# Mixture-of-experts stage of a two-layer transformer kernel: routing weights sent to DRAM and read back over each expert's partitions, in place of TensorE's spreads

## The chip, the cores and the metric

The kernel runs on one core of one Trainium2 chip. The metric is the device time of one execution in microseconds; the number given for a kernel is the median of several executions. A profile is one execution recorded by the hardware profiler. Engines are named as in the profile: PE (TensorE, with PEld for its weight loads), DVE (VectorE), ACT (ScalarE), POOL (GpSimd) and SP (SyncE, which here only issues transfers).

## The reference

32 samples of 256 tokens with 128 features pass through two layers, each an attention block and a feed-forward block, with a layer norm and a per-sample scale, shift and gate around each. The change lies in the feed-forward block of the first layer, a mixture of experts:

```python
def relu2(x): return jnp.square(jax.nn.relu(x))
# router: 16 experts in 4 groups; the 2 best groups by the sum of their 2 best scores,
# then the 4 best experts in them
scores = jax.nn.sigmoid(x2 @ gate_w.T)
sc = scores + bias_e
...
topk_w = topk_w / (topk_w.sum(-1, keepdims=True) + 1e-20) * 2.5
combine = zeros((T, 16)).at[rows, topk_idx].add(topk_w)
def body(acc, inp):
    wu, wd, cw = inp                       # wu (64, 128), wd (128, 64), cw (T,)
    return acc + cw[:, None] * (relu2(x2 @ wu.T) @ wd.T)
routed = scan(body, 0, (up_w, down_w, combine.T))
shared = relu2(x2 @ shared_up.T) @ shared_down.T      # inner size 256
out = routed + shared
```

## The kernel before

The program is a series of stages: setup, first attention, experts (`moe`), second attention, second feed-forward. A barrier stands between two stages. All 32 samples' tokens stay in SBUF (`x`). The experts' stage takes 16 runs (`RUNS`) of two samples each, so 512 tokens (`W`) in 4 tiles of 128.

In a run the inner features are taken in ten blocks `u` of 128 (`IT`): blocks 0 and 1 are the shared expert, blocks 2 to 9 are two routed experts each (j = u - 2, experts 2j and 2j+1, 64 partitions each). For a block, PE multiplies the normalised tokens `hT` into `pU` (`pe_up`), ACT takes the relu into `r` and the square into `q` (into `a` for the shared expert), DVE multiplies `q` by the routing weights (`dve_weigh`) into `a`, and PE multiplies `a` back and adds up in `pD` (`pe_down`). The weight of a token for an expert must stand on all 64 partitions of that expert. Before, this is done by PE: DVE writes the weights [token, expert] as two f16 halves (high part and rest) into `cwp`, PE transposes them (`pe_turn_weights`), ACT copies them to `cwT` (`act_take_weights`), and for each routed block PE multiplies `cwT` by a matrix of zeros and ones, `sel`, into `pC` (`pe_spread`), which `dve_weigh` reads.

The routing itself is a chain on DVE: `dve_scores`, `dve_groups`, `dve_group_ranks`, `dve_chosen`, `dve_weights`, laid out between the `dve_weigh` of the run before. Around it stand `dve_normalise`, PE's transposes of the normalised tokens (`pe_front`), ACT's scale and shift (`act_modulate`), the router's product (`pe_route`) and ACT's exponential (`act_exp`). At a run's end ACT applies the gate (`act_gate`), PE transposes back (`pe_back`) and DVE adds to `x` (`dve_add`).

The order of the work on every engine is written out by hand in one loop per engine; each engine works strictly in that order, and waits on semaphores whose counts are written out too. SP issues in this stage only the weight loads of the last stage (`ahead(sp)`), and is idle after that.

Of the kernel before, what the change touches and what calls it, by code (L numbers as in the profile page):

```python
# [7 lines left out]
F32 = mybir.dt.float32  # L8
# [924 lines left out]
def moe(nc, c, weights, ahead):  # L933


    with ExitStack() as ctx:
# [4 lines left out]
        def sem(name):  # L941
# [7 lines left out]
        RSTEPS = 32  # L949
# [3 lines left out]
        sel = sb('sel', [P, RT, P], F16)  # L953
        lt4 = sb('lt4', [P, NG, NG])
        xn = sb('xn', [P, T4, D])
        hT = [sb(f'hT{k}', [D, W]) for k in range(2)]
        s, cw = (sb(x, [P, T4, E]) for x in ('s', 'cw'))
# [7 lines left out]
        cwp = sb('cwp', [P, T4, P], F16)  # L965
        cwT = [sb(f'cwT{k}', [P, W], F16) for k in range(2)]
# [33 lines left out]
        def pe_route(pe, n):  # L1000
            pe.wait_ge(s_hT, n + 1)
            if n >= 1:
                pe.wait_ge(s_cw, n)
            for t in range(T4):
                last = pe.matmul(pR[:, t * E:(t + 1) * E], hT[n % 2][:, t * P:(t + 1) * P], gT[:, :], start=True, stop=True)
            last.then_inc(s_lg, 1)

        def pe_turn_weights(pe, n):
            pe.wait_ge(s_rt, RSTEPS * (n + 1))
            out = pR[:, BANK // 2:BANK].bitcast(F16)  # L1010
            for t in range(T4):
                last = pe.transpose(out[:, t * P:(t + 1) * P], cwp[:, t, :], c.id16[:, :])
            last.then_inc(s_cT, 1)

        def pe_up(pe, n, u):
            if u == 0:
                pe.wait_ge(s_hT, n + 1)
            if n or u >= 2:
                pe.wait_ge(s_r, IT * n + u - 1)
            t = weights_of(u)  # L1020
            pe.matmul(pU[u % 2][:, :], uT[:, t * P:(t + 1) * P], hT[n % 2][:, :], start=True, stop=True).then_inc(s_up, 1)  # L1021

        def pe_spread(pe, n, u):
            j = u - ST
            if j == 0:
                pe.wait_ge(s_cw, n + 1)
            if n or j >= 2:
                pe.wait_ge(s_a, RT * n + j - 1)
            pe.matmul(pC[j % 2][:, :], sel[:, j, :], cwT[n % 2][:, :], start=True, stop=True).then_inc(s_cb, 1)
# [20 lines left out]
        def _(pe):  # L1050
# [11 lines left out]
            pe.wait_ge(s_k, 4)  # L1062
            for n in range(-1, RUNS + 1):
                if 0 <= n < RUNS:
                    pe_up(pe, n, 0)
                if 0 <= n - 1 < RUNS:
                    pe_down(pe, n - 1, 7)
                if 0 <= n < RUNS:
                    pe_up(pe, n, 1)
                if 0 <= n - 1 < RUNS:  # L1070
                    pe_down(pe, n - 1, 8)
                if 0 <= n < RUNS:
                    pe_turn_weights(pe, n)
                    pe_up(pe, n, 2)
                    pe_spread(pe, n, 2)
                if 0 <= n - 1 < RUNS:
                    pe_down(pe, n - 1, 9)
                if 0 <= n + 1 < RUNS:
                    pe_front(pe, n + 1)
                if 0 <= n < RUNS:  # L1080
                    pe_up(pe, n, 3)
                    pe_spread(pe, n, 3)
                    pe_down(pe, n, 0)
                    pe_up(pe, n, 4)
                    pe_spread(pe, n, 4)
                    pe_down(pe, n, 1)
                if 0 <= n + 1 < RUNS:
                    pe_route(pe, n + 1)
                if 0 <= n < RUNS:
                    pe_up(pe, n, 5)  # L1090
                    pe_spread(pe, n, 5)
                if 0 <= n - 1 < RUNS:
                    pe_back(pe, n - 1)
                if 0 <= n < RUNS:
                    pe_down(pe, n, 2)
                    for u in range(6, IT):
                        pe_up(pe, n, u)
                        pe_spread(pe, n, u)
                        pe_down(pe, n, u - 3)
# [62 lines left out]
        def dve_weights(dve, n):  # L1162
            base = RSTEPS * n
            dve.wait_ge(s_rt, base + 25)
            dve.scalar_tensor_tensor(cw[:, :, :], rep[:, :, 0:E], TAKEN, s[:, :, :], ALU.is_equal, ALU.mult).then_inc(s_rt, 1)
# [31 lines left out]
        def _(dve):  # L1197
# [6 lines left out]
            for n in range(-1, RUNS + 1):  # L1204
                if 0 <= n - 1 < RUNS:
                    dve_weigh(dve, n - 1, 9)
                if 0 <= n < RUNS:
                    dve_weights(dve, n)
                if 0 <= n + 1 < RUNS:
                    dve_normalise(dve, n + 1)  # L1210
# [8 lines left out]
                if 0 <= n + 1 < RUNS:  # L1219
                    dve_scores(dve, n + 1)  # L1220
# [4 lines left out]
                if 0 <= n + 1 < RUNS:  # L1225
                    dve_groups(dve, n + 1)
# [4 lines left out]
                if 0 <= n + 1 < RUNS:  # L1231
                    dve_group_ranks(dve, n + 1)
# [4 lines left out]
                if 0 <= n + 1 < RUNS:  # L1237
                    dve_chosen(dve, n + 1)
# [3 lines left out]
        def act_modulate(act, n):  # L1242
            if n >= 2:
                act.wait_ge(s_up, IT * (n - 1))
            act.wait_ge(s_xT, n + 1)
            for m in range(S2):
                last = act.activation(hT[n % 2][:, m * N:(m + 1) * N], pX[:, m * N:(m + 1) * N], ACT.Identity, scale=c.mod[:, 0, 4, n * S2 + m:n * S2 + m + 1], bias=c.mod[:, 0, 3, n * S2 + m:n * S2 + m + 1])
            last.then_inc(s_hT, 1)

        def act_exp(act, n):  # L1250
            act.wait_ge(s_lg, n + 1)
            if n >= 1:
                act.wait_ge(s_rt, RSTEPS * (n - 1) + 26)
# [19 lines left out]
        def act_take_weights(act, n):  # L1273
            act.wait_ge(s_cT, n + 1)
            if n >= 2:
                act.wait_ge(s_cb, RT * (n - 1))
            act.activation(cwT[n % 2][:, :], pR[:, BANK // 2:BANK].bitcast(F16), ACT.Copy).then_inc(s_cw, 1)

# [9 lines left out]
        def _(act):  # L1288
            for n in range(-1, RUNS + 1):
                if 0 <= n < RUNS:  # L1290
# [3 lines left out]
                    act_take_weights(act, n)  # L1294
# [7 lines left out]
                if 0 <= n + 1 < RUNS:  # L1302
                    act_modulate(act, n + 1)
# [5 lines left out]
                if 0 <= n + 1 < RUNS:  # L1309
                    act_exp(act, n + 1)  # L1310
# [7 lines left out]
        def _(gp):  # L1318
            gp.memset(sel[:, :, :], 0.0).then_inc(s_k, 1)
            gp.memset(lt4[:, :, :], 1.0).then_inc(s_k, 1)  # L1320
            for k in range(2):
                gp.wait_ge(s_k, 2 + k)
                m = sel[:, :, :].rearrange('r t (x i) -> r t x i', i=EI)
                gp.affine_select(out=m, in_=m, compare_op=ALU.not_equal, fill=1.0, base=k * E, pattern=[[2, RT], [1, 2], [0, EI]], channel_multiplier=-1).then_inc(s_k, 1)
# [3 lines left out]
            gp.memset(cwp[:, :, 2 * E:], 0.0).then_inc(s_km, 1)  # L1328
# [765 lines left out]
```

## Time and profile before

| | us |
|---|---|
| median of 3 executions | 2152.71 (2152.59 to 2153.12) |
| profiled execution, its own time | 2151.95 |
| span of its profile | 2150.1 |
| PE busy | 2047.2 (95%) |
| DVE busy | 1650.3 (77%) |
| ACT busy | 1438.3 (67%) |
| POOL busy | 618.3 (29%) |

The profile's times count from the start of the span; "busy" is the time in which an engine executed an instruction, overlaps counted once. The experts' stage has its first matmul at 1002.3 us and its last at 1354.45 us. A wait is put down to the instruction that ended last before it.

### The profile page before, as it was taken

Reading aid. Unit: us, or ns where it says so; the run is one execution under the profiler, and the core shown is the slowest. Engines: PE = TensorE matmul, PEld = TensorE weight load, DVE = VectorE, ACT = ScalarE, POOL = GpSimd, SP = SyncE. Lnnn points to the kernel's source line nnn. Section 1 sums busy time; section 2 is a strip of 40 time slices with the busy share of each in tenths; the row PEclk is TensorE's granted clock in tenths of the full one; section 3 lists DMA queues with packets and bytes.
Section 4 is the critical chain, followed back from the end, with each engine's and each line's share of the span. In section 5 each row is a group of like instructions: output and inputs, shape, how many; then the busy total and the mean of one; then the engine's idle time right before and its main releaser. Section 6 shows DMA issues by size and latency. Waiting matters only on the chain. (4 is left out here: it accounts for less than half of the span.)

```text
span 2150.1 us, 40463 instructions
## 1 busy us (share of the span) xinstructions
PE 2047.2 (95%) x14885; PEld 1372.3 (64%) x14885; DVE 1650.3 (77%) x4015; ACT 1438.3 (67%) x1931; POOL 618.3 (29%) x862
## 2 busy tenths in 40 slices
PE   3899999999999999997999999799999996999998
PEld 1577777777777777775444444577777773444443
DVE  3888888888888888874566665577777776999997
ACT  1687877778887777873666666466666663555554
POOL 1345444544544454552000000133333331000000
PEclk9999999999999999997999999899999997999999
DMA  5000000000000000001000000000000000000000
GB/s 165 21 21 21 21 11 21 21 21 21 21 21 11 21 21 21 21 21 55 1 0 1 1 1 1 1 2 2 2 2 2 2 2 1 10 16 11 15 11 20
DMA packets 32834, 35.30 MB, mean 16 GB/s; under 512 B 6864, under 2 KB 26496, under 8 KB 32640
## 3 DMA queue, kind: packets, MB, share of 16 engines
q1 hardware_dynamic: 32640, 32.73, 5.8%
q8 instruction: 120, 1.97, 0.4%
q14 instruction: 74, 0.61, 0.1%
HBM read 11.75 MB, written 4.19 MB: 7 GB/s over the span
## 5 line engine op out<-in xcount | busy, mean ns | idle before, releaser
L864 POOL TENSOR_SCALAR_AFFINE_SELECT pr<-pr 128x512 f32<-128x512 f32 x256 | 202.2, 813 | 370.7 <-ACT pr L795 370.7
L422 PE MATMUL a_pO<-va,pr 128*128 128x66 f32 x2048 | 304.6, 272 | 1.9 <-POOL pr L864 1.5
L422 PEld LDWEIGHTS a_pO<-va,pr 128*128 128x128 f32 x2048 | 273.7, 193 | 18.9 <-issue 15.4
L1628 ACT ACTIVATE c_pr<-c_pS 128x1536 f32<-128x1536 f32 x128 | 186.0, 1453 | 119.3 <-PE c_pS L1440 119.3
L1683 POOL TENSOR_SCALAR_AFFINE_SELECT c_pr<-c_pr 128x512 f32<-128x512 f32 x256 | 158.0, 641 | 265.4 <-DVE c_pr L1548 265.4
L761 ACT ACTIVATE sq<-a_pW 128x512 f32<-128x512 f32 x192 | 114.4, 597 | 145.4 <-PE a_pW L363 142.7
L789 ACT ACTIVATE th<-a_pS 128x1536 f32<-128x1536 f32 x128 | 185.9, 1453 | 30.1 <-PE a_pS L407 29.6
L423 PE MATMUL a_pO<-va,pr 128*128 128x66 f32 x1024 | 199.0, 276 | 0.0
L795 ACT ACTIVATE pr<-th 128x1536 f32<-128x1536 f32 x128 | 190.5, 1488 | 3.1
L407 PE MATMUL a_pS<-qs,k 128*128 128x512 f16 (+1 forms) x1024 | 187.3, 326 | 0.9 <-issue 0.9
L1548 DVE TENSOR_SCALAR c_pr<-c_pr 128x1536 f32<-128x1536 f32 x128 | 122.6, 958 | 78.4 <-ACT c_pr L1628 78.4
L1021 PE MATMUL b_pU<-b_hT,b_uT 128*128 128x512 f32 x320 | 168.8, 610 | 0.0
L1039 PE MATMUL b_pD<-b_a,b_dT 128*128 128x512 f32 x320 | 163.1, 593 | 0.0
L407 PEld LDWEIGHTS a_pS<-qs,k 128*128 128x128 f16 x1024 | 98.7, 98 | 99.7 <-issue 35.9
L1187 DVE TENSOR_TENSOR b_a<-b_q,b_pC 128x512 f32<-128x512 f32 x128 | 87.8, 686 | 96.1 <-ACT b_q L1271 96.0
L1258 ACT ACTIVATE b_r<-b_pU 128x512 f32<-128x512 f32 x160 | 95.4, 596 | 95.6 <-PE b_pU L1021 95.6
L423 PEld LDWEIGHTS a_pO<-va,pr 128*128 128x128 f32 x1024 | 156.6, 193 | 0.0
L872 POOL TENSOR_TENSOR as<-on 128x128 f32<-128x128 f32 x256 | 116.6, 466 | 109.7 <-PE a_pW L444 95.0
L643 POOL TENSOR_TENSOR qp<-qg,qp 128x1024 f16<-128x1024 f32 x64 | 136.7, 2137 | 25.2 <-ACT qp L771 25.2
L582 DVE TENSOR_TENSOR qg<-a_pW,a_gam 128x512 f32<-128x512 f32 x192 | 131.4, 685 | 10.5 <-ACT sq L761 7.9
L634 DVE RECIPROCAL rl<-a_pO 128x4 f32<-128x4 f32 x256 | 45.0, 176 | 120.5 <-PE a_pO L423 120.5
L363 PE MATMUL a_pW<-a_wq,hT 128*128 128x512 f32 x256 | 125.7, 615 | 1.3 <-DVE qs L651 0.7
(259 smaller groups left out, 4509.1 us busy)
## 6 DMA issues: line engine op xcount, KB each, us to landing
k<-k SPq DMA_DIRECT2D x64, 256.0 KB, 3.6
x<-in_L_attn_tokens_dram SPq DMA_DIRECT2D x8, 512.0 KB, 6.8
out_dram<-x SPq DMA_DIRECT2D x16, 256.0 KB, 2.3
d_h<-in_L_ffn_h_w_dram SPq DMA_DIRECT2D x2, 1024.0 KB, 7.4
wmod<-in_L_wmod_dram SPq DMA_DIRECT2D x2, 384.0 KB, 4.0
d_w<-in_L_ffn_w_w_dram SPq DMA_DIRECT2D x3, 256.0 KB, 3.2
a_wq<-in_L_attn_Wq_dram SPq DMA_DIRECT2D x1, 512.0 KB, 7.1
a_wkv<-in_L_attn_Wkv_dram SPq DMA_DIRECT2D x1, 512.0 KB, 6.9
```

The costliest lines, as they stand in the source:

```text
L407: last = pe.matmul(out, kk[:, h // G2, keys * P:(keys + 1) * P], qs[k][:, h:h + G2, keys * P:N], start=first, stop=not first)
L422: pe.matmul(out, w[:, hh * N + t * P:hh * N + (t + 1) * P], v[:, 0, p, :], start=True, stop=t == 0)
L423: last = pe.matmul(out, w[:, HPG * N + hh * P:HPG * N + (hh + 1) * P], v[:, 1, p, :], start=False, stop=True)
L582: dve.tensor_tensor(qg[n % 2][:, t, cols], pW[BANK_OF[m]][:, :], gam[:, cols], ALU.mult).then_inc(s_qg, 1)
L643: eng.tensor_tensor(to[:, t, :, DH:2 * DH], x.rearrange('p (h d) -> p h d', d=DH), to[:, t, :, 0:DH], ALU.subtract).then_inc(done, 1)
L789: act.activation(th[:, :], pS[:, :], ACT.Tanh, scale=1.0 / SOFTCLAMP).then_inc(s_th, 1)
L795: act.activation(pr[g % 2][:, :], th[:, :], ACT.Exp, scale=SOFTCLAMP * DH ** (-0.5)).then_inc(s_pr, 1)
L864: last = gp.affine_select(out=part, in_=part, compare_op=ALU.is_ge, fill=0.0, base=0, pattern=[[0, HPG], [1, P]], channel_multiplier=-1)
L1021: pe.matmul(pU[u % 2][:, :], uT[:, t * P:(t + 1) * P], hT[n % 2][:, :], start=True, stop=True).then_inc(s_up, 1)
L1039: pe.matmul(pD[:, :], dT[:, t * D:(t + 1) * D], a[(IT * n + u) % 4][:, :], start=u == 0, stop=u == IT - 1).then_inc(s_dn, 1)
L1628: act.activation(pr[g][:, :, :], pS[:, :, 0:N + P], ACT.Exp, scale=float(1.0 / np.sqrt(np.float32(DQ)))).then_inc(s_ex, 1)
L1683: last = gp.affine_select(out=part, in_=part, compare_op=ALU.is_ge, fill=0.0, base=0, pattern=[[0, HPG], [1, P]], channel_multiplier=-1)
```

## The change

The spread by PE is taken out. In its place:

- DVE writes the weights as f32 into `cwp` (32 columns for each tile of tokens, 16 of them used) and transposes them with its own transpose, in blocks of 32 by 32, into `cwT`: block row k holds the experts of the tokens 32k to 32k+31 of every tile.
- SP, in a loop over the runs, waits for `cwT` and for the reads of the run before, issues 4 transfers that write `cwT` to a buffer in DRAM (`by_expert`, ordered by expert), waits until they have landed, and issues 8 transfers that read the rows of two experts each back into `cwB[n % 2][:, j, :]`, each expert's row of 512 weights on 64 partitions. Each of the 8 has a semaphore of its own, `s_cw[j]`, and `dve_weigh` waits for it.
- The routing of a run is done one run earlier: PE's `pe_front` and `pe_route`, ACT's `act_modulate` and `act_exp` and DVE's routing chain now stand for run n+2 where they stood for n+1. `hT` has three buffers, `s` two.
- `pU` has four banks of PSUM instead of two (the two of `pC` are free), so `pe_up` may run further ahead of ACT.

The core of the diff:

```diff
+        cwp, cwT = (sb(x, [P, T4, SQ]) for x in ('cwp', 'cwT'))
+        cwB = [sb(f'cwB{k}', [P, RT, W]) for k in range(2)]
+        by_expert = nc.dram_tensor('b_by_expert', (E, T4, P // SQ, SQ), F32, kind='Internal').ap()
...
         @block.sync
         def _(sp):
             ahead(sp)
+            for n in range(RUNS):
+                sp.wait_ge(s_cT, n + 1)
+                if n >= 1:
+                    for j in range(RT):
+                        sp.wait_ge(s_cw[j], 16 * n)
+                for j in range(P // SQ):
+                    sp.dma_start(by_expert[:, :, j, :], cwT[SQ * j:SQ * j + E, :, :]).then_inc(s_cd, 16)
+                sp.wait_ge(s_cd, 16 * P // SQ * (n + 1))
+                if n >= 2:
+                    sp.wait_ge(s_a, RT * (n - 1))
+                rows = by_expert.rearrange('(j y) t k r -> j y (t k r)', y=2)
+                for j in range(RT):
+                    sp.dma_start(cwB[n % 2][:, j, :], rows[j].unsqueeze(1).broadcast_to((2, EI, W))).then_inc(s_cw[j], 16)
...
-        def pe_turn_weights(pe, n):
-            pe.wait_ge(s_rt, RSTEPS * (n + 1))
-            out = pR[:, BANK // 2:BANK].bitcast(F16)
-            for t in range(T4):
-                last = pe.transpose(out[:, t * P:(t + 1) * P], cwp[:, t, :], c.id16[:, :])
-            last.then_inc(s_cT, 1)
...
-        def pe_spread(pe, n, u):
-            ...
-            pe.matmul(pC[j % 2][:, :], sel[:, j, :], cwT[n % 2][:, :], start=True, stop=True).then_inc(s_cb, 1)
...
-            dve.scalar_tensor_tensor(cw[:, :, :], cw[:, :, :], ROUTED, tot[:, :].unsqueeze(2).broadcast_to((P, T4, E)), ALU.mult, ALU.mult).then_inc(s_rt, 1)
+            dve.scalar_tensor_tensor(cwp[:, :, 0:E], cw[:, :, :], ROUTED, tot[:, :].unsqueeze(2).broadcast_to((P, T4, E)), ALU.mult, ALU.mult).then_inc(s_rt, 1)
             dve.wait_ge(s_rt, base + 30)
             if n >= 1:
-                dve.wait_ge(s_cT, n)
-            dve.tensor_copy(cwp[:, :, 0:E], cw[:, :, :]).then_inc(s_rt, 1)
-            dve.wait_ge(s_rt, base + 31)
-            dve.tensor_tensor(cwp[:, :, E:2 * E], cw[:, :, :], cwp[:, :, 0:E], ALU.subtract).then_inc(s_rt, 1)
+                dve.wait_ge(s_cd, 16 * P // SQ * n)
+            dve.transpose(cwT[:, :, :].rearrange('p t r -> p (t r)'), cwp[:, :, :].rearrange('p t e -> p (t e)')).then_inc(s_cT, 1)
 
         def dve_weigh(dve, n, u):
             j = u - ST
             dve.wait_ge(s_sq, IT * n + u + 1)
-            dve.wait_ge(s_cb, RT * n + j + 1)
+            dve.wait_ge(s_cw[j], 16 * (n + 1))
             if n or u >= 4:
                 dve.wait_ge(s_dn, IT * n + u - 3)
-            dve.tensor_tensor(a[(IT * n + u) % 4][:, :], q[j % 4][:, :], pC[j % 2][:, :], ALU.mult).then_inc(s_a, 1)
+            dve.tensor_tensor(a[(IT * n + u) % 4][:, :], q[j % 4][:, :], cwB[n % 2][:, j, :], ALU.mult).then_inc(s_a, 1)
```

The first place is PE in the middle of the stage, from one run to the next. Before, its rows there are (L1021 is `pe_up`, L1039 `pe_down`, L1012 `pe_turn_weights`, L1029 `pe_spread`, L997 `pe_front`, L1005 `pe_route`):

```order
L1039 MATMUL b_pD<-b_a,b_dT 128x512
L1012 MATMUL b_pR<-id,b_cwp 128x128 x4
L1021 MATMUL b_pU<-b_hT,b_uT 128x512
L1029 MATMUL b_pC<-b_cwT,b_sel 128x512
L1039 MATMUL b_pD<-b_a,b_dT 128x512
L997 MATMUL b_pX<-id,b_xn 128x128 x4
L1021 MATMUL b_pU<-b_hT,b_uT 128x512
L1029 MATMUL b_pC<-b_cwT,b_sel 128x512
```

Of the change the same place reads (L1030 is `pe_up`, L1040 `pe_down`, L1013 `pe_front`):

```order
L1040 MATMUL b_pD<-b_a,b_dT 128x512
L1030 MATMUL b_pU<-b_hT,b_uT 128x512
L1040 MATMUL b_pD<-b_a,b_dT 128x512
L1013 MATMUL b_pX<-id,b_xn 128x128 x4
L1030 MATMUL b_pU<-b_hT,b_uT 128x512
```

The spreads and the transposes of the weights are gone, and nothing stands in their place on PE.

The second place is SP behind the weight loads of the last stage, of the change (before, SP has no row here); a row's brackets name the semaphores that it waits for, and the names are the written and the read tensor:

```order
L1700 DMA d_w3s<-in_L_ffn_w_s_dram 128x1
L997 DMA b_by_expert<-b_cwT 64x1x32 [waits b_cT]
L997 DMA b_by_expert<-b_cwT 64x1x32 x3
L1003 DMA b_cwB<-b_by_expert 128x1x512 [waits b_cd]
L1003 DMA b_cwB<-b_by_expert 128x1x512 x7
L997 DMA b_by_expert<-b_cwT 64x1x32 [waits b_cw4,b_cw3,b_cw5,b_cw2,b_cw6,b_cw1,b_cw7,b_cw0,b_cT]
L997 DMA b_by_expert<-b_cwT 64x1x32 x3
L1003 DMA b_cwB<-b_by_expert 128x1x512 [waits b_cd]
```

A run's four writes wait for all eight reads of the run before, and its eight reads wait for its four writes, so the runs' transfers do not overlap.

The third place is DVE at the stage's start, of the change (L1165 to L1171 end `dve_weights`, L1105 is `dve_scores`): behind the first run's weights stands the whole routing of the second run.

```order
L1165 RECIPROCAL b_tot<-b_tot 128x4 [waits b_rt]
L1167 SCALAR_TENSOR_TENSOR b_cwp<-b_cw,b_tot 128x4x16 [waits b_rt]
L1171 STREAM_TRANSPOSE b_cwT<-b_cwp 128x128 [waits b_rt]
L1105 TENSOR_SCALAR b_s<-b_s 128x64 [waits b_ex]
L1107 RECIPROCAL b_s<-b_s 128x64 [waits b_rt]
```

Before, the normalising of the second run's tokens (L103) and the first `dve_weigh` (L1187) stood right behind the first run's weights:

```order
L1173 SCALAR_TENSOR_TENSOR b_cw<-b_cw,b_tot 128x64 [waits b_rt]
L1177 CAST b_cwp<-b_cw 128x4x16 [waits b_rt]
L1179 TENSOR_TENSOR b_cwp<-b_cw,b_cwp 128x4x16 [waits b_rt]
L103 TENSOR_SCALAR b_xn<-x,mv,rs 128x128 [waits b_xT]
L103 TENSOR_SCALAR b_xn<-x,mv,rs 128x128 x3
L1187 TENSOR_TENSOR b_a<-b_q,b_pC 128x512 [waits b_cb,b_sq] x2
```

A second routing chain has come between the first run's weights and the work that follows them.

## Rows read from the trace of the kernel before

**Rows 1.** Stretches: length, then each engine's busy us, PE's clock, DMA share, GB/s

```profile
1110.00:1130.00 20.00, 20.00 (x67) 9.84 (x66) 13.13 (x58) 13.04 (x26) 0.00 (x0) 1.00 0.00 0
1130.00:1150.00 20.00, 20.00 (x68) 9.78 (x66) 13.09 (x58) 13.04 (x25) 0.00 (x0) 1.00 0.01 2
1360.00:1400.00 40.00, 33.22 (x330) 24.96 (x331) 23.05 (x47) 22.59 (x25) 12.00 (x22) 0.85 0.00 1
```

**Rows 2.** Timeline of PE, mid-stage: start us, length us, then the instructions merged

```profile
1113.69 1.02 PE L1021 MATMUL b_pU<-b_hT,b_uT 128*128 128x512 f32 x2
1114.55 0.38 PE L1029 MATMUL b_pC<-b_cwT,b_sel 128*128 128x512 f16 x1
1114.77 1.02 PE L1039 MATMUL b_pD<-b_a,b_dT 128*128 128x512 f32 x2
...
1123.14 1.02 PE L1021 MATMUL b_pU<-b_hT,b_uT 128*128 128x512 f32 x2
1124.00 1.02 PE L1039 MATMUL b_pD<-b_a,b_dT 128*128 128x512 f32 x2
1124.86 0.39 PE L1012 MATMUL b_pR<-id,b_cwp 128*128 128x128 f16 x4
1125.08 1.08 PE L1021 MATMUL b_pU<-b_hT,b_uT 128*128 128x512 f32 x2
1125.99 0.38 PE L1029 MATMUL b_pC<-b_cwT,b_sel 128*128 128x512 f16 x1
...
1145.80 0.39 PE L1012 MATMUL b_pR<-id,b_cwp 128*128 128x128 f16 x4
```

**Rows 3.** Groups of the stage by line and shape: busy us, mean ns, idle before

```profile
L1187 DVE TENSOR_TENSOR b_a<-b_q,b_pC 128x512 f32<-128x512 f32 x128 | 87.8, 686 | 96.1 <-ACT b_q L1271 96.0
...
L1029 PE MATMUL b_pC<-b_cwT,b_sel 128*128 128x512 f16 x128 | 48.8, 381 | 0.0
```

**Rows 4.** Timeline at the stage's start, with the last step of the first run's weights

```profile
1012.63 0.20 DVE L1111 TENSOR_SCALAR b_s<-b_s 128x64 f32<-128x64 f32 x1 [4.07 <-ACT b_s L1254]
...
1018.89 0.23 DVE L1179 TENSOR_TENSOR b_cwp<-b_cw,b_cwp 128x64 f16<-128x64 f32 x1
...
1021.81 1.06 PE L997 MATMUL b_pX<-id,b_xn 128*128 128x128 f32 x4
```

**Rows 5.** Timeline at the stage's end: the last weighing and the gate

```profile
1351.14 0.69 DVE L1187 TENSOR_TENSOR b_a<-b_q,b_pC 128x512 f32<-128x512 f32 x1 [1.16 <-ACT b_q L1271]
...
1353.56 0.84 ACT L1284 ACTIVATE b_og<-b_pD,mod 128x256 f32<-128x256 f32 x2 [2.45 <-PE b_pD L1039]
```

**Rows 6.** Timeline of SP in the first attention: two transfers issued

```profile
525.69 0.46 SPq L306 DMA_DIRECT2D k<-k  x1
526.20 0.60 SPq L307 DMA_DIRECT2D k<-k  x1
```

**Rows 7.** DMA issues: count, KB each, median us from issue to landing

```profile
k<-k SPq DMA_DIRECT2D x64, 256.0 KB, 3.6
out_dram<-x SPq DMA_DIRECT2D x16, 256.0 KB, 2.3
...
b_gn<-in_L_ffn_gate_w_dram SPq DMA_DIRECT2D x1, 8.0 KB, 2.7
```

**Rows 8.** DMA of 554 to 562 us, holding two k transfers of 64 x 4 KB

```profile
GB/s 0 0 0 0 0 0 0 0 164 205 266 246 123 246 61 246 430 389 246 0 0 0 0 0 0 0 0 0 0 0 0 0 0 0 0 0 0 0 0 0
DMA packets 160, 0.52 MB, mean 66 GB/s; under 512 B 32, under 2 KB 32, under 8 KB 160
## 3 DMA queue, kind: packets, MB, share of 16 engines
q1 hardware_dynamic: 160, 0.52, 26.0%
```

**Rows 9.** DMA of 1007 to 1007.5 us, packets of 2 KB alone

```profile
q1 hardware_dynamic: 66, 0.14, 84.2%
```

**Rows 10.** DMA of 1012 to 1012.5 us, packets of 2 KB alone

```profile
DMA packets 97, 0.20 MB, mean 397 GB/s; under 512 B 0, under 2 KB 0, under 8 KB 97
...
q1 hardware_dynamic: 97, 0.20, 106.0%
```

**Rows 11.** The instructions of pe_up: ns min/median/max, first and last start

```profile
L1021 PE MATMUL b_pU<-b_hT,b_uT x320: 592/592/1201, 1012.2 to 1349.2; 128*128 128x512 f32 x160
```

More of the change, by code:

```diff
@@ L948, in moe @@
         ROW = E + EG
-        RSTEPS = 32
+        RSTEPS = 30
+        SQ = 32
         HIGH, TAKEN = 3.0e38, -3.0e38
@@ L952, in moe @@
         uT, dT, gT = (sb('uT', [D, IT * P]), sb('dT', [P, IT * D]), sb('gT', [D, E]))
-        sel = sb('sel', [P, RT, P], F16)
         lt4 = sb('lt4', [P, NG, NG])
         xn = sb('xn', [P, T4, D])
-        hT = [sb(f'hT{k}', [D, W]) for k in range(2)]
-        s, cw = (sb(x, [P, T4, E]) for x in ('s', 'cw'))
+        hT = [sb(f'hT{k}', [D, W]) for k in range(3)]
+        s = [sb(f's{k}', [P, T4, E]) for k in range(2)]
+        cw = sb('cw', [P, T4, E])
         sc, mk, rep = (sb(x, [P, T4, ROW]) for x in ('sc', 'mk', 'rep'))
@@ L1002, in pe_route @@
             if n >= 1:
-                pe.wait_ge(s_cw, n)
+                pe.wait_ge(s_ex, n)
             for t in range(T4):
-                last = pe.matmul(pR[:, t * E:(t + 1) * E], hT[n % 2][:, t * P:(t + 1) * P], gT[:, :], start=True, stop=True)
+                last = pe.matmul(pR[:, t * E:(t + 1) * E], hT[n % 3][:, t * P:(t + 1) * P], gT[:, :], start=True, stop=True)
             last.then_inc(s_lg, 1)
-        def pe_turn_weights(pe, n):
-            pe.wait_ge(s_rt, RSTEPS * (n + 1))
-            out = pR[:, BANK // 2:BANK].bitcast(F16)
-            for t in range(T4):
-                last = pe.transpose(out[:, t * P:(t + 1) * P], cwp[:, t, :], c.id16[:, :])
-            last.then_inc(s_cT, 1)
         def pe_up(pe, n, u):
@@ L1017, in pe_up @@
                 pe.wait_ge(s_hT, n + 1)
[L1018 to L1019 removed]
+            if n or u >= 4:
+                pe.wait_ge(s_r, IT * n + u - 3)
             t = weights_of(u)
[L1021 to L1029 removed]
+            pe.matmul(pU[(IT * n + u) % 4][:, :], uT[:, t * P:(t + 1) * P], hT[n % 3][:, :], start=True, stop=True).then_inc(s_up, 1)
         def pe_down(pe, n, u):
@@ L1061, in _ @@
             pe.wait_ge(s_taken, len(turns))
-            pe.wait_ge(s_k, 4)
-            for n in range(-1, RUNS + 1):
+            for n in range(-2, RUNS + 1):
                 if 0 <= n < RUNS:
@@ L1203, in _ @@
             dve.wait_ge(s_km, 4)
-            for n in range(-1, RUNS + 1):
+            for n in range(-2, RUNS + 1):
                 if 0 <= n - 1 < RUNS:
                     dve_weigh(dve, n - 1, 9)
-                if 0 <= n < RUNS:
-                    dve_weights(dve, n)
                 if 0 <= n + 1 < RUNS:
-                    dve_normalise(dve, n + 1)
+                    dve_weights(dve, n + 1)
+                if n == -2:
+                    dve_normalise(dve, 0)
+                    dve_normalise(dve, 1)
+                elif 0 <= n < RUNS - 2:
+                    dve_normalise(dve, n + 2)
                 if 0 <= n < RUNS:
@@ L1288, in _ @@
         def _(act):
-            for n in range(-1, RUNS + 1):
+            for n in range(-2, RUNS + 1):
                 if 0 <= n < RUNS:
@@ L1318, in _ @@
         def _(gp):
-            gp.memset(sel[:, :, :], 0.0).then_inc(s_k, 1)
             gp.memset(lt4[:, :, :], 1.0).then_inc(s_k, 1)
[L1321 to L1324, printed above, removed]
+            gp.wait_ge(s_k, 1)
             gp.affine_select(out=lt4[:, :, :], in_=lt4[:, :, :], compare_op=ALU.is_gt, fill=0.0, base=0, pattern=[[1, NG], [-1, NG]], channel_multiplier=0).then_inc(s_km, 1)
```

82 lines of the change are left out of this document (34 added, 48 removed).

## The prediction

> **What bounds the kernel now.** I read three views in this order. The stretches of the experts' stage come first: in two windows of 20 us PE is busy for all 20.00 us at a granted clock of 1.00, which is 2.4 GHz, while DVE and ACT have some 13 us of work and the DMA engines none [rows 1]. The reader is to see that every other engine has slack and transfers have the whole machine to themselves. The timeline of PE shows what a run is made of: the same row, the transposes of the weights, starts at 1124.86 and at 1145.80 us, so a run takes 20.94 us, and 16 runs make 335 us of the 2150 [rows 2]. Third, the groups: DVE's weighing waits 96.0 us in the stage for ACT's squares, behind which PE stands again [rows 3]. So the stage goes at PE's pace, and whatever leaves PE is gained, as long as nothing else takes longer than PE's run.
>
> **What leaves PE.** A spread takes a slot of 1114.77 - 1114.55 = 0.22 us between a `pe_up` and a `pe_down` [rows 2]; its mean of 381 ns overlaps the next matmul [rows 3]. Eight make 1.74 us. The transposes of the weights take 0.22 us (1124.86 to 1125.08), and the `pe_up` behind them has a slot of 0.91 us where others have 0.86 (1123.14 to 1124.00) [rows 2]. Together 2.0 us of a run, so PE's run becomes 18.94 us. ACT loses one copy, DVE a cast and a subtraction for one transpose of 128x128; neither is near 18.94 us.
>
> **What comes in its place.** SP's loop is a closed chain, and I price one turn of it.
> - Four writes: SP needs 0.46 to 0.60 us for an issue [rows 6], so the fourth goes out 1.6 us after the first. It moves little; small or DRAM-bound transfers land 2.3 to 2.7 us after issue [rows 7]; I take 2.3. That is 3.9 us, and no read may start before.
> - Start of the reads: the two k transfers of rows 7 need 3.6 us each for 64 packets, of which data is some 2 us in the burst of rows 8; about 1.5 us are latency. Sum so far 5.4 us.
> - Eight reads: each writes 128 rows of 2 KB, 256 KB, so 1024 packets and 2.1 MB a run. How long they take hangs on how many of the 16 DMA engines carry them.
>
> That last point decides everything. What the trace shows of sharing out: the two k transfers have 64 rows of 4 KB each on both sides, and left 128 packets of data and 32 small ones, 16 for each transfer, while their burst reached 430 GB/s [rows 8]. So a transfer whose outer dimension is 64 has its rows dealt to all 16 engines, with one closing packet on each. The new reads differ in one thing: the destination has 128 partitions outside, but the source is written as 2 rows, each repeated 64 times, so its outer dimension is 2. If engines are dealt equal pieces of the outer dimension of both sides, there are only 2 equal pieces to deal, each of 64 packets, and all eight reads come to lie on two engines. No row of the trace has a transfer with an outer dimension under 16, so the rows can't show it; I choose this reading, because the closing packets show that the deal is made by whole shares of the instruction's rows, and the share here can't be finer than the source's two rows without cutting through the repeat.
>
> The Trainium skill states this as a rule (DMA: Bandwidth & Descriptors, "Why a DMA increments its semaphore by 16 and not by 1"): the number of engines is the largest up to 16 that divides both sides' slowest dimension, and on SP's queue it is the lowest-numbered ones that work; its "Rules for kernel authors" warns of an outermost dimension under 16. By that rule each read runs on engines 0 and 1 alone, the same two every time. Rows 8 agree for 64 (16 closing packets); no run here shows it for 2 so far.
>
> **The price of two engines.** Packets of 2 KB alone: 97 of them in 0.5 us took 106.0% of 16 engines, 0.5 x 16 x 1.06 / 97 = 87 ns each, and by rate 397 / 16 = 24.8 GB/s, 83 ns [rows 10]. I take 85 ns. Each of two engines has 8 x 64 = 512 packets a run: 43.5 us. A turn is 5.4 + 43.5 = 48.9 us, against 18.94 of PE's. PE's own run may even fall to half clock for its idling (`pe_up` takes 592 ns at full and up to 1201 at half clock [rows 11]): 2 x 18.94 = 37.9 us still hides beneath 48.9. The double buffer doesn't help, since this is throughput; nor does choosing the weights a run ahead, which covers one turn's latency and not a queue that grows.
> - First write: the weights of the first run are done at 1019.1 us before [rows 4]; one step less and the transpose leave about 1019.0.
> - Last read landed: 1019.0 + 16 x 48.9 = 1801.4 us. The last weighing, at 1351.14 us before [rows 5], waits for it: +450.3.
> - Tail and next stage: the last `pe_down`, the transposes back and the first matmuls of the second attention now run at the lower clock from the start (that stretch has 0.85 before [rows 1]): I put 3 us, chosen between 0 and 6.
>
> Sum +453 us. The profiled execution took 2151.95 us by its own time, 0.8 below the median 2152.71, so 2152.7 + 453 = **2606 us**.
>
> **Bounds.** The fastest slice of the k burst, 430 GB/s, is 26.9 GB/s an engine, 76 ns for 2 KB [rows 8]: turn 44.3, kernel 2533. In another half microsecond 66 packets took 84.2%, 102 ns [rows 9]: turn 57.6, kernel 2746. The k packets as a whole, 26.0% of 16 engines in 8 us for 128 of 4 KB, are 130 ns for 2 KB [rows 8]: turn 72, kernel 2976; their engines also waited for one another's SBUF rows, so I hold it for an outer end. That 64 packets read the same row of DRAM has no row at all; it could cost or save. The transpose on DVE and its wait for the writes are hidden either way: in a turn of 48.9 us DVE has 13.
>
> **Rivals.**
> 1. *All sixteen engines share each read, or the pairs differ from read to read: faster.* Then the reads need 1024 x 85 / 16 = 5.4 us, the turn 10.8 us, under 18.94, and PE stays the bound. Gain 16 x 2.0 = 32.0 us. Against it stands the start: DVE's chain from scores to weights takes 6.4 us (1012.63 to 1019.1) [rows 4], and now a second one stands before the normalising of the run that `pe_front` needs. `pe_front`, at 1021.81 before, starts at about 1019.0 + 6.1 + 1.1 = 1026.2, and PE's low clock lasts longer: together 5.5 us; 0.9 us of spreads were hidden in that start already; back come 1.3 us, since one transpose and routing more lies in the idle start. 32.0 - 5.5 - 0.9 + 1.3 = 26.9: **2126 us**. For it: the 430 GB/s burst. Against it: the source's form. It decides as soon as a turn is below 18.94 us, that is from about 7 engines on (5.4 + 1024 x 0.085 / 7 = 17.8).
> 2. *Sixteen engines, but the reads land one after another*: 3.9 + 8 x 3.6 [rows 7] = 32.7 us a turn, 1019 + 523 = 1542, +191: **2344 us**. Against it: two k transfers issued 0.5 us apart [rows 6] were both over in the one burst of rows 8.
> 3. *Two engines, and rereading one DRAM row makes a packet dearer*: at 102 ns 2746 us, in the first case's own range.
>
> **How the numbers follow.** Two engines, with any price of a packet, 0.84: its own range 2520 to 2870 (packets of 74 to 117 ns, the bounds above without the outermost) holds 95 in 100 of it. Sixteen or changing pairs 0.12, of which almost nothing comes out within 0.2% of before, some 4 us, which is about what a measurement of this kernel can tell from no change. One after another 0.04. Time 2606 us, that of the likeliest; range 2520 to 2870, which holds 0.84 x 0.95 = 0.80 of all and so need not reach the others. Faster 0.12, same 0.01, slower 0.87.
>
> **What the changed profile would show.** In the experts' stage a DMA share near 2/16 = 0.11 to 0.13 without a gap, about 43 GB/s; DVE's weighing released by the reads of `cwB` and not by ACT, most of DVE's idle time in front of it; PE busy well under 90% and its clock at 0.50 for most of the stage; the reads' landing times spread up to over 40 us, and SP waiting for them at the first write. The stage some 785 us long. A share of 0.3 in bursts of 6 to 10 us with PE still at 20.00 of 20 would show rival 1; reads that land at 3.6 us steps, rival 2. The prediction is wrong if engines are dealt single rows whatever the form of the source; it is off in size if a packet on a lonely engine takes another time than in a burst of sixteen.

## The result, and the profile after

The changed kernel takes 2589.36 us (2588.71 to 2589.5) against 2152.65 us of before measured beside it: a ratio of 1.2028, 95% interval 1.2007 to 1.2049, slower by 437 us. Forecast were 2606 us, in a range of 2520 to 2870.

The page of the changed kernel: first busy time of the engines (share of the span, instructions), then the span in 40 slices with PE's clock, the DMA share and GB/s, and one row of its costliest groups.

```profile
PE 2172.5 (84%) x14693; PEld 1385.4 (54%) x14693; DVE 1653.1 (64%) x3999; ACT 1436.0 (55%) x1915; POOL 615.6 (24%) x859
...
PE   3999999999999997655566656564999999799999
...
PEclk9999999999999996888877777776999999899999
DMA  4100010001000001111111111110000000000000
GB/s 137 25 18 18 17 25 18 18 18 26 17 17 18 19 24 52 46 46 42 46 45 44 46 43 45 46 42 32 2 2 2 2 2 2 1 9 17 13 13 17
...
L1179 DVE TENSOR_TENSOR b_a<-b_q,b_cwB 128x512 f32<-128x512 f32 x128 | 88.6, 692 | 524.1 <-DMA b_cwB<-b_by_expert 265.9
```

The experts' stage now fills slices 16 to 28. The DMA row holds a flat 1 in slices 16 to 27, a tenth of the sixteen engines, with 42 to 52 GB/s and never more. DVE's weighing waits 524 us, where it waited 96 us behind ACT [rows 3]; 265.9 us of it are put down to the reads, and 220.5 us to "issue", which names no cause, but at the same pace of 5.20 us as the rows below show. A stretch in the stage is to be set beside [rows 1]; under it, of ten microseconds in the middle of a run's reads, the DMA view:

```profile
1200.00:1250.00 50.00, 29.43 (x59) 11.37 (x57) 13.53 (x57) 14.03 (x26) 0.00 (x0) 0.81 0.12 45
```

```profile
DMA packets 250, 0.50 MB, mean 50 GB/s; under 512 B 4, under 2 KB 4, under 8 KB 250
## 3 DMA queue, kind: packets, MB, share of 16 engines
q1 hardware_dynamic: 250, 0.50, 13.1%
```

13.1% of sixteen engines is 2.1 engines; 16 x 10 x 0.131 / 250 = 84 ns for a packet. PE is busy for 29 us in 50, where it was for 20 in 20. SP's timeline gives the turn of the loop, DVE's the pace of the reads:

```profile
1021.57 2.58 SPq L997 DMA_DIRECT2D b_by_expert<-b_cwT  x4
1025.38 30.17 SPq L1003 DMA_DIRECT2D b_cwB<-b_by_expert  x8
1069.45 2.51 SPq L997 DMA_DIRECT2D b_by_expert<-b_cwT  x4
1073.19 29.82 SPq L1003 DMA_DIRECT2D b_cwB<-b_by_expert  x8
1117.20 2.50 SPq L997 DMA_DIRECT2D b_by_expert<-b_cwT  x4
```

```profile
1229.85 0.69 DVE L1179 TENSOR_TENSOR b_a<-b_q,b_cwB 128x512 f32<-128x512 f32 x1 [4.52 <-DMA b_cwB<-b_by_expert]
1235.06 0.69 DVE L1179 TENSOR_TENSOR b_a<-b_q,b_cwB 128x512 f32<-128x512 f32 x1 [4.52 <-DMA b_cwB<-b_by_expert]
1240.26 0.69 DVE L1179 TENSOR_TENSOR b_a<-b_q,b_cwB 128x512 f32<-128x512 f32 x1 [3.91 <-issue]
...
1788.29 0.69 DVE L1179 TENSOR_TENSOR b_a<-b_q,b_cwB 128x512 f32<-128x512 f32 x1 [4.41 <-issue]
```

From write to write a turn is 47.8 us (47.6 to 48.4, mean 47.9): 3.8 us until the first read goes out, 8 reads at 5.20 us each (41.6), and a remainder of 2.4 us for the start of the first read and the landing of the last. The last row is the stage's last weighing; it stood at 1351.14 us [rows 5], so it comes 437.2 us later, and the span grew by 437.5.

### The profile page after: what moved, and what is told of

Read it like the earlier page. It is cut to its first block and busy times, and to the rows that moved or that the text cites. A ratio compares the mean times of both kernels' runs of the same rounds, so it can differ in the third digit from the quotient of the medians.

```text
span 2587.6 us, 40277 instructions
## 1 busy us (share of the span) xinstructions
PE 2172.5 (84%) x14693; PEld 1385.4 (54%) x14693; DVE 1653.1 (64%) x3999; ACT 1436.0 (55%) x1915; POOL 615.6 (24%) x859
## 5 line engine op out<-in xcount | busy, mean ns | idle before, releaser
L1040 PE MATMUL b_pD<-b_a,b_dT 128*128 128x512 f32 x320 | 236.1, 829 | 271.5 <-DVE b_a L1179 271.5
L1179 DVE TENSOR_TENSOR b_a<-b_q,b_cwB 128x512 f32<-128x512 f32 x128 | 88.6, 692 | 524.1 <-DMA b_cwB<-b_by_expert 265.9
L1040 PEld LDWEIGHTS b_pD<-b_a,b_dT 128*128 128x128 f32 x320 | 64.7, 240 | 426.7 <-DVE b_a L1179 400.3
L1030 PE MATMUL b_pU<-b_hT,b_uT 128*128 128x512 f32 x320 | 225.3, 798 | 0.0
```

Of the source, the lines that this page charges most:

```text
L1030: pe.matmul(pU[(IT * n + u) % 4][:, :], uT[:, t * P:(t + 1) * P], hT[n % 3][:, :], start=True, stop=True).then_inc(s_up, 1)
L1040: pe.matmul(pD[:, :], dT[:, t * D:(t + 1) * D], a[(IT * n + u) % 4][:, :], start=u == 0, stop=u == IT - 1).then_inc(s_dn, 1)
```

## The experiments

Each is the changed kernel with one edit unless said otherwise. Experiments 3 and 6 to 9 are one execution each, so a few us in their times mean little; ratios are to before, measured beside them. Rival A is that rereading one DRAM row is what costs; rival B that SP's queue is the limit and not the engines.

**1. One expert a read.** The same bytes and the same repeats, but both outer dimensions are 64.

```diff
-                    sp.dma_start(cwB[n % 2][:, j, :], rows[j].unsqueeze(1).broadcast_to((2, EI, W))).then_inc(s_cw[j], 16)
+                    for y in range(2):
+                        sp.dma_start(cwB[n % 2][y * EI:(y + 1) * EI, j, :], rows[j][y:y + 1].broadcast_to((EI, W))).then_inc(s_cw[j], 16)
```

The waits on `s_cw` count in 32 instead of 16.

> Edit: each read of 128 partitions is cut into two of 64, one expert's row repeated 64 times, so that the outer dimension is 64 on both sides; the same 2.1 MB a run and the same rereading of each DRAM row 64 times. Theory (a transfer is dealt to as many engines as both outer dimensions can be cut into equally; 2 in the changed kernel): all 16 engines work, a turn of SP's loop is 3.8 us of writes, 16 issues of about 0.5 us and 2 to 3 us to the last landing, 14 to 15 us, below PE's 18.9; PE is the bound again, its run 18.94 us, kernel 2126 us (2120 to 2135), DMA share near 0.3. Rival A (rereading one DRAM row is what is slow, whatever the number of engines): the same row is read as often, so the turn stays near 47.8 us and the kernel at 2589. Rival B (SP's queue can hold only so many transfers, and each costs its 5.2 us): 16 transfers make it no better, 2589 or slower.

Measured: 2125.44 us (2124.34 to 2128.02), 0.9878 of before (0.9862 to 0.9895). The same data arrive, each DRAM row still read 64 times, from the same queue in twice as many transfers, and 464 us are gone: rivals A and B both fall. In its profile, two rows of PE's timeline, one run apart, then the DMA view of 1200 to 1219 us, then SP's timeline:

```profile
1217.83 0.60 PE L1014 MATMUL b_pX<-id,b_xn 128*128 128x128 f32 x4
1236.79 0.60 PE L1014 MATMUL b_pX<-id,b_xn 128*128 128x128 f32 x4
```

```profile
DMA packets 1641, 2.14 MB, mean 113 GB/s; under 512 B 616, under 2 KB 616, under 8 KB 1640
## 3 DMA queue, kind: packets, MB, share of 16 engines
q1 hardware_dynamic: 1640, 2.13, 37.1%
```

```profile
1018.79 2.56 SPq L997 DMA_DIRECT2D b_by_expert<-b_cwT  x4
1022.58 10.08 SPq L1004 DMA_DIRECT2D b_cwB<-b_by_expert  x16
1034.94 2.49 SPq L997 DMA_DIRECT2D b_by_expert<-b_cwT  x4
```

PE's run is 18.96 us (18.94 by the prediction's working). A turn of SP's loop is 16.2 us, of which 10.1 go into issuing 16 transfers: 2.8 us below PE's run; 14 to 15 us were expected, and 10.8 us in the prediction's rival with eight reads.

**2. Two reads a run.**

```diff
-                rows = by_expert.rearrange('(j y) t k r -> j y (t k r)', y=2)
-                for j in range(RT):
-                    sp.dma_start(cwB[n % 2][:, j, :], rows[j].unsqueeze(1).broadcast_to((2, EI, W))).then_inc(s_cw[j], 16)
+                rows = by_expert.rearrange('(j y) t k r -> y j (t k r)', y=2)
+                for y in range(2):
+                    sp.dma_start(cwB[n % 2][y * EI:(y + 1) * EI, :, :], rows[y:y + 1].broadcast_to((EI, RT, W))).then_inc(s_cw[y], 16)
```

> Edit: two reads a run instead of eight, each of 64 partitions with all eight rows of one half (even or odd experts), outer dimension 64 on both sides, 1 MB each; each weighing waits for both. Theory (engines by the outer dimension): both reads on 16 engines, 1024 packets of 81 ns over 16 engines are 5.2 us, the turn 3.8 + 0.5 + 5.2 + 2.4, about 12 us; PE the bound, 2126 us, at most 2 us beside the first experiment; SP has 14 issues fewer, which costs nothing either way as SP has time. Rival A (rereading a row): 2589. Rival B (each transfer costs 5.2 us): the turn would be 3.8 + 2.4 + 10.4 = 16.6 us, also under 18.9, so this run doesn't test B; the first does.

Measured: 2131.62 us, 0.9905 (0.989 to 0.9919), 6 us more than the first experiment where at most 2 were expected. DVE's timeline at the start and the DMA view of 1200 to 1219 us:

```profile
1038.23 2.50 DVE L1180 TENSOR_TENSOR b_a<-b_q,b_cwB 128x512 f32<-128x512 f32 x4 [9.58 <-DMA b_cwB<-b_by_expert]
```

```profile
DMA packets 1378, 2.15 MB, mean 113 GB/s; under 512 B 352, under 2 KB 352, under 8 KB 1376
## 3 DMA queue, kind: packets, MB, share of 16 engines
q1 hardware_dynamic: 1376, 2.13, 54.2%
```

The first weighing needs both megabytes and waits 9.58 us for them, 1.96 us of which reach PE; from first matmul to last weighing the stage is 2.0 us longer than in the first experiment (325.7 against 323.7). Another 2.7 us of the 5.5 us between the two profiles' spans lie ahead of the stage: its first matmul came at 1004.26 us here and at 1001.59 in the first experiment, in work that the edit doesn't touch. The last 0.8 us lie behind it, unexplained. And a packet costs more: 54.2% of sixteen engines for the bytes that took 37.1% there.

**3. Four outer pieces instead of two.**

```diff
-        by_expert = nc.dram_tensor('b_by_expert', (E, T4, P // SQ, SQ), F32, kind='Internal').ap()
+        by_expert = nc.dram_tensor('b_by_expert', (E, 2, T4, P // SQ, SQ), F32, kind='Internal').ap()
...
+                    for d in range(2):
+                        sp.dma_start(by_expert[:, d, :, j, :], cwT[SQ * j:SQ * j + E, :, :]).then_inc(s_cd, 16)
...
-                rows = by_expert.rearrange('(j y) t k r -> j y (t k r)', y=2)
+                rows = by_expert.rearrange('(j y) d t k r -> j (y d) (t k r)', y=2)
...
-                    sp.dma_start(cwB[n % 2][:, j, :], rows[j].unsqueeze(1).broadcast_to((2, EI, W))).then_inc(s_cw[j], 16)
+                    sp.dma_start(cwB[n % 2][:, j, :], rows[j].unsqueeze(1).broadcast_to((4, EI // 2, W))).then_inc(s_cw[j], 16)
```

> Edit: each expert's row is written to DRAM twice (8 small writes a run instead of 4) and each read takes 4 rows, each repeated 32 times: the outer dimension of the source is 4 instead of 2, everything else of the reads as in the changed kernel. Theory (engines by the outer dimension): 4 engines, 32 packets each a read, 2.6 us a read; turn 8 x 0.6 + 1.8 for the writes, 8 x 2.6 = 20.8 for the reads, 2.4 latency, 29.8 us; PE still waits; kernel 2589 - 16 x (47.8 - 29.8) = 2301 us; DMA share in a read burst 4/16 = 0.25. Rival A (rereading one DRAM row): each row is reread half as often; if that were the cost the reads would fall to something between 41.6 and 20.8 us a run but the DMA share would stay at 0.12. Rival B (a transfer's fixed price of 5.2 us): 47.8 + 2.4, kernel about 2627.

Measured: 2274.87 us. DVE's weighings come 2.60 us apart, half of 5.20, and in 1082 to 1100 us the DMA view says four engines, 25.6% of sixteen:

```profile
1088.69 0.69 DVE L1180 TENSOR_TENSOR b_a<-b_q,b_cwB 128x512 f32<-128x512 f32 x1 [1.88 <-DMA b_cwB<-b_by_expert]
1091.30 0.69 DVE L1180 TENSOR_TENSOR b_a<-b_q,b_cwB 128x512 f32<-128x512 f32 x1 [1.92 <-DMA b_cwB<-b_by_expert]
```

```profile
q1 hardware_dynamic: 872, 1.74, 25.6%
```

The kernel is 26 us under the forecast because it takes 4.7 us from the first of the eight small writes to the first read, and not 6.6: the turn is 28.1 us on average instead of 29.8. The share of 25.6% speaks against rival A, which had 0.12, and a transfer's fixed price (rival B) is excluded once more.

**4. Reads in the first two runs only.** Fourteen runs weigh with old routing weights.

```diff
-            for n in range(RUNS):
+            for n in range(2):
                 sp.wait_ge(s_cT, n + 1)
...
-                dve.wait_ge(s_cd, 16 * P // SQ * n)
+                dve.wait_ge(s_cd, 16 * P // SQ * min(n, 2))
...
-            dve.wait_ge(s_cw[j], 16 * (n + 1))
+            dve.wait_ge(s_cw[j], 16 * min(n + 1, 2))
```

> Edit: SP makes its writes and reads only for the first two runs; later runs weigh with what stands in the two buffers, so the routing weights of 14 of the 16 runs are left wrong (the work of all engines but the DMA queue is unchanged). Theory: shows PE's run of 18.94 us without any transfer beside it and the price of the start: the first two turns are 47.8 us each on two engines, so runs 0 and 1 end at about 1021.6 + 95.6 = 1117, the other 14 go at PE's 18.94 us: about 1117 + 14 x 18.94 + 5 = 1387, 401 less than 1788: kernel about 2188 us. If transfers slowed PE or DVE in SBUF, the steady run here would be shorter than in the first experiment; I expect the same within 0.05 us.

Measured: 2179.8 us, 1.0127 of before (1.0112 to 1.0142), 8 us under the forecast. PE's timeline in its steady part, without a transfer beside it:

```profile
1216.86 0.60 PE L1013 MATMUL b_pX<-id,b_xn 128*128 128x128 f32 x4
1235.82 0.60 PE L1013 MATMUL b_pX<-id,b_xn 128*128 128x128 f32 x4
```

18.96 us again. The 2.1 MB a run of the first experiment take nothing measurable from PE, DVE or ACT: from 1200 to 1219 us DVE is busy 13.26 us with them and 13.30 without, ACT 13.65 and 13.65.

**5. The start mended**, on top of the first experiment.

```diff
                 if n == -2:
                     dve_normalise(dve, 0)
                     dve_normalise(dve, 1)
-                elif 0 <= n < RUNS - 2:
+                elif n == -1:
+                    dve_normalise(dve, 2)
+                elif 1 <= n < RUNS - 2:
                     dve_normalise(dve, n + 2)
```

> Edit: the first experiment (one expert a read, 16 engines), and DVE normalises the third run's tokens before the second run's routing and not behind it. Theory (rival 1 of the prediction as it now stands: 16 x 2.0 us gained, some 5.5 us lost at the start, where PE waited 4.72 us for these tokens at half clock): PE's transposes of them start near 1021 instead of 1026.04 us and the clock rises earlier; DVE's first weighing stays at 1026.1 and its result is wanted a little later, so 4 to 5 us come back: 2121 us (2118 to 2124) against 2125.4. Rival: the first weighing at 1026.1 is late then and the wait only moves from the tokens to PE's third product with the down weights: at most 1 us gained.

Measured: 2121.39 us (2118.56 to 2123.15), 0.985 of before (0.9836 to 0.9863), the fastest kernel of the study; the interval just touches the first experiment's. Within the stage it is plain. The first matmul, the transposes of the third run's tokens, and the last weighing, of the first experiment:

```profile
1001.59 2.37 PE L1060 MATMUL b_pU<-id,b_un 128*128 128x128 f32 x10 [5.13 <-PEq L246]
...
1026.04 1.12 PE L1014 MATMUL b_pX<-id,b_xn 128*128 128x128 f32 x4 [4.72 <-DVE b_xn L103]
...
1325.29 0.69 DVE L1180 TENSOR_TENSOR b_a<-b_q,b_cwB 128x512 f32<-128x512 f32 x1 [0.94 <-ACT b_q L1267]
```

and of the fifth:

```profile
1004.78 2.37 PE L1060 MATMUL b_pU<-id,b_un 128*128 128x128 f32 x10 [5.13 <-PEq L246]
...
1023.24 0.60 PE L1014 MATMUL b_pX<-id,b_xn 128*128 128x128 f32 x4
...
1029.54 1.12 PE L1041 MATMUL b_pD<-b_a,b_dT 128*128 128x512 f32 x2 [0.51 <-DVE b_a L1180]
...
1321.28 0.69 DVE L1180 TENSOR_TENSOR b_a<-b_q,b_cwB 128x512 f32<-128x512 f32 x1 [0.94 <-ACT b_q L1269]
```

The transposes come 18.5 us into the stage instead of 24.5, without a wait and already at full clock (0.60 us for four, not 1.12), and the stage is 7.2 us shorter. Only 4 us show in the time, since this execution entered the stage 3.2 us later. The rival's wait is there, but small: PE waits 0.51 us for the first weighing.

**6. The same reads from POOL's queue.** The read loop stands in POOL's program, with the same waits.

```diff
+            for n in range(RUNS):
+                gp.wait_ge(s_cd, 16 * P // SQ * (n + 1))
+                if n >= 2:
+                    gp.wait_ge(s_a, RT * (n - 1))
+                rows = by_expert.rearrange('(j y) t k r -> j y (t k r)', y=2)
+                for j in range(RT):
+                    gp.dma_start(cwB[n % 2][:, j, :], rows[j].unsqueeze(1).broadcast_to((2, EI, W))).then_inc(s_cw[j], 16)
```

> Edit: the changed kernel with its eight reads of outer dimension 2 unchanged, but issued by POOL instead of SP (POOL is idle in this stage). Theory (what is dealt equally is the outer dimension, and which engines get it belongs to the queue): the Trainium skill says that from POOL's queue a transfer on few engines goes to consecutive engines from a cursor that moves on, and from SP's to the lowest-numbered. Then each read still takes 64 packets of 81 ns, 5.2 us, but the eight run side by side on 16 engines: turn 3.8 + about 1 us an issue, 8 + 5.2 + 2.4, some 19 us, kernel 2126 to 2170, DMA share in a burst over 0.5. Rival (the shape limits to the same two engines from any queue): turn 47.8 or more, kernel 2589 or more, DMA share 0.12.

Measured: 2165.59 us. The DMA view of 1100 to 1140 us:

```profile
DMA  8742001000344588999999751000100143557999
GB/s 152 142 128 75 4 0 17 10 7 0 12 65 101 125 198 193 195 169 165 218 179 166 190 121 45 0 0 10 15 8 0 22 57 89 121 170 194 195 173 149
...
q0 software_dynamic: 7621, 3.79, 49.9%
...
b_cwB<-b_by_expert POOLq DMA_DIRECT2D x16, 256.0 KB, 11.8
```

Reads of the very same form now reach 218 GB/s with all engines at work in the middle of the burst. So the two outer pieces alone don't tie them to one pair; the pair is that of SP's queue. The turn is 21.3 us on average, above PE's 18.96 and above the 19 expected, and the price of a read is why. On POOL's queue (q0) the same bytes take twice the engine time: 16 x 40 x 0.499 = 319 us for 3.79 MB are 173 ns for 2 KB, the queue's many small packets included, against 84 ns on SP's queue. 64 rows at that price on one engine are 11 us, and a read lands 11.8 us after its issue. With 3.8 us for the writes and seven issues of 0.8 us ahead of the last read that gives 21.1 us.

**7. Odd reads from ACT's queue.**

```diff
-                for j in range(RT):
+                for j in range(0, RT, 2):
                     sp.dma_start(cwB[n % 2][:, j, :], rows[j].unsqueeze(1).broadcast_to((2, EI, W))).then_inc(s_cw[j], 16)
...
+        def act_reads(act, n):
+            act.wait_ge(s_cd, 16 * P // SQ * (n + 1))
+            if n >= 2:
+                act.wait_ge(s_a, RT * (n - 1))
+            rows = by_expert.rearrange('(j y) t k r -> j y (t k r)', y=2)
+            for j in range(1, RT, 2):
+                act.dma_start(cwB[n % 2][:, j, :], rows[j].unsqueeze(1).broadcast_to((2, EI, W))).then_inc(s_cw[j], 16)
```

> Edit: the changed kernel with its reads unchanged, the four of even j issued by SP and the four of odd j by ACT at the end of the run before. Theory (two engines, the lowest-numbered ones from either queue): the 512 packets an engine stay, turn 47.8, kernel 2575 to 2640; ACT may wait while it issues, hidden beneath the reads. Rival B (SP's queue, not the engines, is what passes one read in 5.2 us): two queues pass two at once, turn 3.8 + 4 x 5.2 + 2.4 = 27 us, kernel 2256, DMA share 0.25 in a burst.

Measured: 2593.95 us. Two queues (q1 is SP's, q10 ACT's) share what one had, in 1100 to 1150 us:

```profile
q1 hardware_dynamic: 861, 1.12, 6.2%
q10 hardware_dynamic: 541, 1.09, 5.9%
```

6.2 and 5.9% make the same two engines' worth. Rival B is excluded directly: a second queue onto the same engines gives nothing.

**8. Half the bytes.** The routing weights are one f16 value from the routing's last step on, which changes their precision.

```diff
-        cwp, cwT = (sb(x, [P, T4, SQ]) for x in ('cwp', 'cwT'))
-        cwB = [sb(f'cwB{k}', [P, RT, W]) for k in range(2)]
+        cwp, cwT = (sb(x, [P, T4, SQ], F16) for x in ('cwp', 'cwT'))
+        cwB = [sb(f'cwB{k}', [P, RT, W], F16) for k in range(2)]
```

(`by_expert` is F16 too.)

> Edit: the changed kernel with the weights as one f16 value from the last step of the routing on (transposed, written, read back and multiplied as f16), so rows of 1 KB instead of 2 KB; number of packets, engines and order unchanged; the routing weights lose precision. Theory (the two engines' bytes are the price): 1 KB takes somewhat over half of 81 ns, 45 ns; turn 3.8 + 512 x 0.045 + 2.4 = 29.2 us, kernel 2589 - 16 x 18.6 = 2291. Rival (each packet or each repeat of a row has a fixed price): turn near 47.8, kernel 2589.

Measured: 2290.6 us. Reads come 2.78 us apart, 43 ns a packet of 1 KB, and a turn is 29.2 us: on two engines it is bytes that are paid for.

**9. Different rows.** The reads take 2 x 64 different rows of the tokens, so the routed experts are weighed with tokens.

```diff
-                rows = by_expert.rearrange('(j y) t k r -> j y (t k r)', y=2)
+                rows = tokens.rearrange('(y b) (i m f) d -> m y b i (f d)', y=2, m=2, f=4)
...
-                    sp.dma_start(cwB[n % 2][:, j, :], rows[j].unsqueeze(1).broadcast_to((2, EI, W))).then_inc(s_cw[j], 16)
+                    sp.dma_start(cwB[n % 2][:, j, :], rows[j % 2][:, 2 * (j // 2):2 * (j // 2) + 2].rearrange('y b i w -> y (b i) w')).then_inc(s_cw[j], 16)
```

> Edit: the changed kernel with each read taking 2 x 64 different rows of 2 KB of the input tokens (outer dimension 2, rows 4 KB apart) instead of 2 rows repeated 64 times; the expert blocks are weighed with tokens and not with routing weights, so the routed output is left wrong. Theory (two engines, 81 ns a packet whatever it reads): turn 47.8 us, kernel 2589 (2580 to 2600). Rival A in its weak form (rereading one row of DRAM makes each packet dearer or cheaper, beside the number of engines): another turn; if the repeat costs, shorter, each 10 ns a packet being 16 x 512 x 0.01 = 82 us.

Measured: 2600.44 us, 11 us more than the changed kernel and 0.4 us beyond the forecast. DVE's rows inside a run are 5.21 us apart, as good as before; a turn is 48.6 us on average (48.0 to 49.9) where it was 47.9, which over 16 turns is the whole difference:

```profile
1232.75 0.69 DVE L1179 TENSOR_TENSOR b_a<-b_q,b_cwB 128x512 f32<-128x512 f32 x1 [4.52 <-DMA b_cwB<-in_L_attn_tokens_dram]
1237.97 0.69 DVE L1179 TENSOR_TENSOR b_a<-b_q,b_cwB 128x512 f32<-128x512 f32 x1 [4.53 <-DMA b_cwB<-in_L_attn_tokens_dram]
```

Rereading one DRAM row costs nothing in the pace of the reads; rival A falls in its weak form too. Why the turns grew between the runs' reads stays open.

## Why the prediction was right

**Two engines** carried the reads, which was the step that decided. The share of 13.1%, the 5.20 us a read, the halving with four outer pieces and the end of it with 64 show it from four sides. Other explanations were tried and fell: rereading a row (experiments 1, 3 and 9), a fixed price of a transfer or a packet (1, 3 and 8) and SP's queue by itself (1 and 7). The prediction argued it from the source's two rows and held 0.84 for it. The Trainium skill's rule (DMA: Bandwidth & Descriptors, "Why a DMA increments its semaphore by 16 and not by 1") agrees with the runs for 2, for 4 and for 64 outer pieces; its part on the queues agrees too, a fixed set from SP and ACT (experiment 7) and changing ones from POOL (experiment 6), though no view names the engines.

**The turn** was put at 48.9 us and is 47.8 to 47.9. Its terms: writes to first read 3.9, measured 3.8, in which two misses cancel by luck (the fourth write goes out some 1.9 us after the first and not 1.6, and lands after 1.8 us and not 2.3); data 43.5, measured 41.6, because a packet passes every 81 ns and not 85; latency at the ends 1.5, measured 2.4 as the remainder. From the first write to the last weighing the sixteen turns took 766.7 us where 782.4 were forecast, 15.7 us less. That is the whole miss of the forecast in the profiled executions (437.4 against 453), since the start and the tail below cancel. The bounds of 76 and 130 ns were wide (that the engines of the k transfers waited for one another, which the prediction gave as a reason for the 130, is shown by no row); the packets of the burst at 1012 us [rows 10] were the right row, and its rate (83 ns) was a better guide to the pace of 81 than its share (87).

**The start** was 2.6 us later than worked out (1021.57 against 1019.0). 2.1 us of it came in with the stage, whose first matmul is at 1004.36 instead of 1002.3, so that wasn't the change's.

**The tail** was mis-sized: 3 us were put on lower clocks, and only 0.3 came (437.5 of span less 437.2 of weighing).

**PE at half clock under the reads** came partly, where the prediction had 0.50 for most of the stage: inside the stage the slices show 0.7 to 0.8. Two rows of PE show both levels, 1.2 and 2.4 GHz, for two matmuls of the same shape: one behind a wait of 3.22 us for a weighing, one after 4 us of work without a wait:

```profile
1188.03 2.08 PE L1040 MATMUL b_pD<-b_a,b_dT 128*128 128x512 f32 x2 [3.22 <-DVE b_a L1179]
...
1222.44 1.02 PE L1030 MATMUL b_pU<-b_hT,b_uT 128*128 128x512 f32 x2
```

It was hidden either way, since the turn is SP's.

**The other signs** came as written: a DMA share of 0.12 with 45 GB/s, and a stage of 787 us (785 forecast). Landing times spread up to 40 us can't be seen, as the profile gives none for these reads; what it shows is SP standing in its issues for 30 us of each turn, a wait that the prediction's price of 0.46 to 0.60 us an issue didn't have. It cost nothing, because SP has nothing else to do.

**What leaves PE**, 2.0 us a run, is confirmed by experiment 1: 20.94 - 18.96 = 1.98. Rival 1's whole sum, 2126 us, was measured at 2125.4, though with sixteen reads and a turn of 16.2 us in place of eight and 10.8. Its cost at the start was real: of 31.7 us that PE gives up in 16 runs the stage kept 25.1 in experiment 1 (348.8 us before, 323.7 in it), and experiment 5 gave the rest back.

So the change's idea holds and its form undid it: experiment 5 keeps 32.3 us in the stage (348.8 us before from first matmul to last weighing, 316.5 in it).

## What to carry to other kernels

Look at the outermost dimension of a transfer's source before pricing it (it is the side that these runs varied below 16; the destination's was 128 or 64): 256 KB dealt to two engines took 5.2 us each in a queue, dealt to sixteen they vanished beneath the matmuls. A flat DMA share of two sixteenths with a waiting engine is how it looked in the profile; the broadcast of two rows was better written as two transfers of one row each. Choosing something a run ahead hides a latency, never a throughput above the run's length, so compare the whole turn of the loop with the run that must cover it.

## What the runs showed of the hardware

- SP is held up in its issues when the reads lie on two engines: eight reads took 30.17 us to issue in the changed kernel (median 5.05 us each, close to the 5.20 us of a read), against 0.6 us each in experiment 1. That a queue is full then is likely, but no view shows it.
- A 2 KB packet took 84 ns with two engines working, about 16 x 19 x 0.371 / 1024 = 110 ns at most in experiment 1 (128 KB a read), and 16 x 19 x 0.542 / 1024 = 161 ns in experiment 2 (1 MB a read); in both, sixteen engines write one half of the partitions with each read. The cause wasn't isolated.
- DVE's transpose of 128x128 f32 takes 0.31 us, less than its cast (0.20) and subtraction (0.23) together before.
- The unchanged first attention ended up to 3.2 us apart between the programs' profiled executions (first matmul of the experts' stage at 1001.59 to 1004.78 us). Differences of 2 us between kernels of this size are better read inside a stage than from the total. The cause is open.
